# Batch 1's score stacks built by selection products, batch 0's maxima subtracted by a product, and a new order of steps

## The chip, the cores and the metric

The kernel runs on one core of a Trainium2 chip. The metric is the device time of one execution in microseconds (us); lower is better. The engines are TensorE (PE, with its weight loads as PEld), VectorE (DVE), ScalarE (ACT), GpSimd (POOL) and SyncE (SP, which issues all transfers; its queue is SPq).

## The reference

16 batches of 256 tokens x 128 channels pass through one attention layer and one mixture-of-experts layer, each between layer norms and with a residual:

```python
qkv = einsum('bnc,ce->bne', layernorm(x), w_qkv)         # 16 heads of 8 channels
attn = softmax(einsum('bhnd,bhmd->bhnm', q, k) / sqrt(128))
x = x + layernorm(einsum('bhnm,bhmd->bhnd', attn, v) @ w_out)
xf = layernorm(x)
rw = weights of the 2 best of 8 experts of xf @ Wr + bias # softmax over the two
ffn = sum_e rw[e] * (silu(xf @ Wg[e]) * (xf @ Wu[e])) @ Wd[e] + silu(xf @ Sg) * (xf @ Su) @ Sd
x = x + layernorm(ffn)
```

## The kernel before

One batch is one unit of work, cut into about 100 named steps. The table `TIMES` gives each step of each batch a tick; every engine runs its own steps in the order of the ticks and waits on semaphores for what they need. So the table is the whole order: a step's place on its engine is its tick, and steps of three or four batches are mixed. A step's name with a batch in brackets, `s1_3(1)`, is what the text below uses.

Attention works with heads in pairs (`s` = 0 to 7, two heads of rows 0 to 47 and 64 to 111). q and k are split in three bf16 parts (`part1`, `part2`, `part3`, on ScalarE, ScalarE and GpSimd, with `rest1` on VectorE), and six products of parts stand as six groups of 8 rows in the stacks `qs` and `ks`: 48 rows per head. Scores are made twice: `s1` (L630) has queries on the output partitions and feeds `max` (L1011), which finds each query's maximum; `s2` (L646) has keys there and feeds `exp` (L860). In `s2` the maxima are subtracted by three more rows of the stacks: `ks` holds -1 there (`load_minus`), `qs` the maxima, split in three by `msplit` (GpSimd), transposed by `maxT` (L684), copied by `max_copy` (L867) and brought in by the transfers of `max_stack` (L558). `pv` (L662) multiplies with v. The score banks `sc` are two; `s1` and `s2` steps take them in turn, so each waits for the `max` or `exp` of the step before the last.

The stacks of a batch are made by transfers: `spill` writes `parts` to DRAM in 6 transfers (L541, L544), `stack` reads it back in 4 (L551, L553). Batch 0's stacks are made without them, since nothing is there to hide the way: `sel1`, `sel2`, `sel3`, `selq` (L739 to L752) multiply `parts[0]` with selection matrices `lay`, and `kl_copy`, `ql_copy`, `kh_copy`, `qh_copy` bring the results to `ks` and `qs`. `lay` lies in the memory of `hidden` and is made by `lay0a`, `lay0b`, `lay1`, `lay2`.

`FILL`, `FILL_SCORES` and `FILL_LAST` put filler products of the identity (L669, L611, L673) ahead of named steps; one filler is two instructions of the trace. One f32 product is two instructions of the trace, a bf16 product one.

## Time and profile before

| | us |
|---|---|
| median of 3 runs | 373.94 |
| lowest and highest | 372.68, 377.52 |
| the profiled execution | 373.3 |
| its span in the trace | 371.5 |
| TensorE busy | 347.3 (93%) |
| VectorE busy | 312.9 (84%) |
| ScalarE busy | 267.4 (72%) |
| GpSimd busy | 200.5 (54%) |
| granted TensorE clock, mean | 0.988 |

The span is the time from the first to the last instruction in the trace; 1.8 us of the execution's time lie around it. Busy shares are means over stages with different limits: the start has attention alone, the middle attention and experts of different batches, the end experts alone.

### The profile page before, as it was taken

The numbers are of one execution on the slowest core, as the hardware profiler recorded it, in microseconds if no ns is written. First come the engines' busy times: TensorE is split into PE (matmuls) and PEld (weight loads), VectorE is DVE, ScalarE is ACT, GpSimd is POOL, SyncE is SP. The second block draws the span as 40 slices with busy tenths as digits, with TensorE's granted clock in tenths as the row PEclk, the third lists the DMA queues.
The fourth block names the chain that finished last, engine by engine and source line by source line (L and its number), as shares of the span: only waits on it lengthen the run. The fifth ranks groups of instructions, "written<-read, shape, count | busy, mean of one in ns | idle before, by whom it ended". The sixth has DMA issues, their size and how long they took to land.

```text
span 371.5 us, 9933 instructions
## 1 busy us (share of the span) xinstructions
PE 347.3 (93%) x3244; PEld 222.8 (60%) x3244; DVE 312.9 (84%) x788; ACT 267.4 (72%) x511; POOL 200.5 (54%) x518
## 2 busy tenths in 40 slices
PE   8987888999999999999998999999999999998892
PEld 7855444454475657575756565665765566677772
DVE  8696588989989999999888999999998987667661
ACT  4752578689779778969885896788778968864522
POOL 7333051424566454776656365754773576767654
PEclk9998799999999999999999999999999999999998
DMA  2256858663377456355566565386364240422210
GB/s 84 66 136 149 209 119 188 146 145 113 108 183 159 142 127 164 79 144 161 131 170 140 145 125 158 103 199 149 86 185 103 66 129 27 123 62 72 58 31 29
DMA packets 59921, 45.64 MB, mean 123 GB/s; under 512 B 8966, under 2 KB 56966, under 8 KB 59870
## 3 DMA queue, kind: packets, MB, share of 16 engines
q1 hardware_dynamic: 59870, 45.00, 48.3%
q8 instruction: 26, 0.43, 0.5%
q14 instruction: 25, 0.20, 0.2%
HBM read 26.69 MB, written 17.81 MB: 120 GB/s over the span
## 4 chain that ended last, share of the span: by engine, by line
PE 59%; issue 10%; DVE 10%; POOL 7%; ACT 5%; DMA 5%; SPq 3%; POOLq 0%; DVEq 0%; ACTq 0%
PE pvp L662 10%; PE bank_d L832 8%; PE bank_d L816 8%; PE sc L646 7%; DVE mx L1011 6%; PE bank_d L817 6%; PE sc L630 5%; PE bank_a L715 3%; PE bank_d L669 2%; PE bank_d L789 2%; POOL hidden L1220 2%; ACT pr L860 2%; PE sc L611 2%; DMA ks<-qk_dram 2%; POOL rstd L1153 1%
## 5 line engine op out<-in xcount | busy, mean ns | idle before, releaser
L1011 DVE TENSOR_REDUCE mx<-sc 128x4 f32<-128x1024 f32 x128 | 154.3, 1217 | 18.7 <-PE sc L630 17.7
L860 ACT ACTIVATE pr<-sc 128x1024 f32<-128x1024 f32 x128 | 130.8, 1024 | 27.4 <-PE sc L646 26.6
L662 PE MATMUL pvp<-pr,va 128*32 128x256 f32 x1024 | 68.5, 385 | 0.0
L816 PE MATMUL bank_d<-x3T,wg_sb 128*128 128x256 f32 x160 | 54.2, 420 | 2.8 <-DVE hidden L1109 1.9
L630 PE MATMUL sc<-ks,qs 48*128 48x256 bf16 x512 | 50.0, 274 | 3.4 <-DVE mx L1011 1.9
L646 PE MATMUL sc<-qs,ks 51*128 51x256 bf16 x512 | 50.1, 276 | 1.8 <-DMA qs<-mT 1.3
L1220 POOL TENSOR_TENSOR hidden<-hidden,rwb 128x256 f32<-128x256 f32 x60 | 42.2, 729 | 11.0 <-DMA rwb<-rw_dram 10.2
L817 PE MATMUL bank_d<-x3T,wu_sb 128*128 128x256 f32 x160 | 47.6, 379 | 0.0
L1153 POOL TENSOR_TENSOR rstd<-vareps,mhalf 128x2 f32<-128x2 f32 x64 | 44.5, 696 | 0.0
L662 PEld LDWEIGHTS pvp<-pr,va 128*32 128x32 f32 x1024 | 26.7, 109 | 25.1 <-issue 12.4
L943 ACT ACTIVATE th<-bank_d 128x256 f32<-128x256 f32 x80 | 30.5, 382 | 14.8 <-PE bank_d L817 12.8
L832 PE MATMUL bank_d<-wd_sb,hidden 128*128 128x128 f32 x320 | 39.2, 278 | 0.4 <-POOL hidden L1220 0.2
L1103 DVE SCALAR_TENSOR_TENSOR ha<-th,bank_d 128x256 f32<-128x256 f32 x80 | 32.3, 406 | 8.6 <-ACT th L943 8.1
L832 PEld LDWEIGHTS bank_d<-wd_sb,hidden 128*128 128x128 f32 x320 | 37.1, 192 | 3.2 <-issue 2.5
L1148 POOL TENSOR_TENSOR vareps<-mv,eps 128x2 f32<-128x2 f32 x64 | 12.5, 195 | 45.3 <-DVE mv L994 42.8
L646 PEld LDWEIGHTS sc<-qs,ks 51*128 51x128 bf16 x512 | 16.1, 95 | 32.7 <-issue 14.5
L816 PEld LDWEIGHTS bank_d<-x3T,wg_sb 128*128 128x128 f32 x160 | 24.1, 188 | 18.9 <-issue 18.3
L1109 DVE SCALAR_TENSOR_TENSOR hidden<-ha,bank_d 128x256 f32<-128x256 f32 x80 | 32.8, 412 | 1.6 <-PE bank_d L832 0.6
L817 PEld LDWEIGHTS bank_d<-x3T,wu_sb 128*128 128x128 f32 x160 | 30.4, 190 | 4.1
L1164 POOL TENSOR_TENSOR parts<-rest,parts 128x512 bf16<-128x512 f32 x16 | 18.5, 1157 | 26.7 <-ACT parts L888 26.7
L630 PEld LDWEIGHTS sc<-ks,qs 48*128 48x128 bf16 x512 | 18.7, 95 | 23.0 <-DVE mx L1011 7.2
L1043 DVE RECIPROCAL rden<-den 128x256 f32<-128x256 f32 x14 | 24.4, 1745 | 2.4 <-DMA den<-pv_dram 2.4
(115 smaller groups left out, 495.7 us busy)
## 6 DMA issues: line engine op xcount, KB each, us to landing
rwb<-rw_dram SPq DMA_DIRECT2D x30, 256.0 KB, 4.3
qk_dram<-parts SPq DMA_DIRECT2D x30, 192.0 KB, 2.7
qs<-qk_dram SPq DMA_DIRECT2D x30, 192.0 KB, 4.1
ks<-qk_dram SPq DMA_DIRECT2D x30, 192.0 KB, 4.6
qk_dram<-parts SPq DMA_DIRECT2D x30, 128.0 KB, 2.5
pv_dram<-pv_sb SPq DMA_DIRECT2D x14, 256.0 KB, 2.4
x_sb<-in_L_attn_x_dram SPq DMA_DIRECT2D x16, 128.0 KB, 2.7
out_dram<-x SPq DMA_DIRECT2D x16, 128.0 KB, 1.8
```

What stands on the lines that cost most here:

```text
L630: mm = pe.matmul(sc[pair][:, u, c, :], q[rows, s, c * P:(c + 1) * P], k[rows, s, :], start=True, stop=True)
L646: mm = pe.matmul(sc[pair][:, u, c, :], k[rows, s, c * P:(c + 1) * P], q[rows, s, :], start=True, stop=True)
L662: mm = pe.matmul(pvp[32 * j:32 * j + 32, g, :], values[:, X * c + 4 * g + j, 32 * tt:32 * tt + 32], pr[:, k, c * N:(c + 1) * N], start=(tt ...
L816: pe.matmul(bank_d[bank][:, 0:N], wg_sb[:, ORDER[n], :], x3T[b % 2][:], start=True, stop=True)
L817: pe.matmul(bank_d[bank][:, N:2 * N], wu_sb[:, ORDER[n], :], x3T[b % 2][:], start=True, stop=True).then_inc(gu_done, 1)
L832: mm = pe.matmul(bank_d[0][:, c * P:(c + 1) * P], src, wd_sb[:, n, :], start=(n == 4), stop=(n == 3))
L860: nc.scalar.activation(pr[:, 2 * s:2 * s + 2, :].rearrange("p k n -> p (k n)"), sc[PAIR["s2", b, s]][:].rearrange("p u c n -> p (u c n)"), ...
L1011: nc.vector.tensor_reduce(mx[b % 2][:, :, :, s].rearrange("p c u -> p u c"), sc[PAIR["s1", b, s]][:], AX.X, ALU.max).then_inc(max_done, 1)
L1103: nc.vector.scalar_tensor_tensor(out=ha[n][:], in0=th[n][:], scalar=1.0, in1=bank_d[BANK[n]][:, 0:N], op0=ALU.add, op1=ALU.mult).then_inc( ...
L1109: nc.vector.scalar_tensor_tensor(out=hb[b % 2][:, ORDER[n], :], in0=ha[n][:], scalar=0.5, in1=bank_d[BANK[n]][:, N:2 * N], op0=ALU.mult, o ...
L1153: nc.gpsimd.tensor_tensor(rstd[L][p][:], vareps[L][p][:], mhalf[:], ALU.pow).then_inc(rstd_done[L], 1)
L1220: nc.gpsimd.tensor_tensor(hw[b % 2][:, n, :].rearrange("p (t g r) -> p t g r", t=TT, g=4), hb[b % 2][:, n, :].rearrange("p (t g r) -> p t ...
```

## The change

- Batch 1 has no `spill` and no `stack`. Eight steps `u0` to `u7` on TensorE make its stacks: each multiplies `parts[1]` with `lay` for two head pairs, the even ones for `ks` into bank `bank_d[0]`, the odd ones for `qs` into `pvp`. Eight copies `uc0` to `uc7` on ScalarE bring them over. `u_j` waits for `uc_(j-2)`; `s1_s(1)` with even `s` waits for `s + 2` copies.
- Batch 0 has no `max_stack`. `maxT(0)` puts the two halves of the maxima at rows 0 and 64, `max_copy(0)` is two copies, and each `s2` step of batch 0 has four products of 48 rows and four more of 24 rows that add `msel` (-1 in the rows of the step's head) times `mT[0]` to the same bank. `msel` is a new table, made by GpSimd.
- `load_minus` waits for all copies of batch 1, and batch 1's `s2` waits for it.
- Every tick of the table is new; fillers are fewer.

The core of the diff:

```diff
-    "maxT": {0: 7},
+    "maxT": {0: 1},
     "qk": {0: 1},
     "sel1": {0: 2},
-    "xT": {0: 17, 3: 4},
+    "xT": {0: 17},
 }
 FILL_SCORES = {
-    ("s1", 0, 2): 1,
-    ("s1", 0, 3): 1,
-    ("s1", 1, 3): 1,
-    ("s1", 1, 4): 2,
-    ("s1", 2, 7): 1,
-    ("s1", 3, 6): 1,
+    ("s1", 2, 1): 2,
+    ("s1", 3, 7): 1,
     ("s2", 0, 0): 2,
-    ("s2", 0, 4): 2,
-    ("s2", 0, 5): 1,
-    ("s2", 1, 3): 2,
+    ("s2", 1, 1): 1,
 }
...
                 sp.wait_ge(kh_copied, 2)
+                sp.wait_ge(unit_copied, 8)
...
-                if (b := due(tick, "spill")) is not None and b:
+                if (b := due(tick, "spill")) is not None and b >= 2:
...
-                if (b := due(tick, "stack")) is not None and b:
+                if (b := due(tick, "stack")) is not None and b >= 2:
...
-                if (b := due(tick, "max_stack")) is not None:
-                    sp.wait_ge(max_copied, b + 1)
+                if (b := due(tick, "max_stack")) is not None and b:
+                    sp.wait_ge(max_copied, b + 2)
...
+                if b == 1 and s % 2 == 0:
+                    pe.wait_ge(unit_copied, s + 2)
...
                 if s == 0:
-                    pe.wait_ge(max_stacked[b % 2], landed(2, b))
                     if b == 0:
+                        pe.wait_ge(max_copied, 2)
+                        pe.wait_ge(msel_done, 6)
+                    else:
+                        pe.wait_ge(max_stacked[b % 2], landed1(2, b))
+                    if b == 1:
                         pe.wait_ge(minus_load, DMA * 2)
...
-                        rows = slice(64 * u, 64 * u + ROWS_MAX)
-                        mm = pe.matmul(sc[pair][:, u, c, :], k[rows, s, c * P:(c + 1) * P], q[rows, s, :], start=True, stop=True)
+                        rows = slice(64 * u, 64 * u + (ROWS_MAX if b else ROWS))
+                        mm = pe.matmul(sc[pair][:, u, c, :], k[rows, s, c * P:(c + 1) * P], q[rows, s, :], start=True, stop=b > 0)
+                    if b == 0:
+                        for u in range(2):
+                            rows = slice(64 * u, 64 * u + 3 * X)
+                            mm = pe.matmul(sc[pair][:, u, c, :], msel[rows, s:s + 1].broadcast_to([3 * X, P]), mT[0][rows], start=False, stop=True)
...
+                for j in range(8):
+                    if due(tick, f"u{j}") is not None:
+
+                        pe.wait_ge(part3_done, 2)
+                        if j < 2:
+                            pe.wait_ge(qh_copied, 2)
+                        else:
+                            pe.wait_ge(unit_copied, j - 1)
+                        bank = bank_d[0][0:WIDTH].rearrange("p (x n) -> p x n", x=2) if j % 2 == 0 else pvp[0:WIDTH]
+                        q = 1 - j % 2
+                        for x in range(2):
+                            for n in range(3):
+                                mm = pe.matmul(bank[:, x, :], lay[:, n, q, 2 * (j // 2) + x, :], parts[1][:, q, n, :], start=(n == 0), stop=(n == 2))
+                        mm.then_inc(unit_done, 1)
+                        if j == 6:
+                            d_empty[0] = (unit_copied, 7)
...
+                for j in range(8):
+                    if due(tick, f"uc{j}") is not None:
+                        act.wait_ge(unit_done, j + 1)
+                        bank = bank_d[0][0:WIDTH].rearrange("p (x n) -> p x n", x=2) if j % 2 == 0 else pvp[0:WIDTH]
+                        dst = qs[1][0:WIDTH] if j % 2 else ks[0:WIDTH, 1]
+                        nc.scalar.copy(dst[:, 2 * (j // 2):2 * (j // 2) + 2, :], bank).then_inc(unit_copied, 1)
```

The new order of the steps at the start, on the engines that the prediction speaks of:

- TensorE: xT(0) qk(0) sel1 v(0) sel2 xT(1) sel3 qk(1) selq xT(2) s1_0(0) s1_1(0) v(1) u0 s1_2(0) u1 s1_3(0) qk(2) u2 s1_4(0) s1_5(0) u3 v(2) u4 s1_6(0) u5 s1_7(0) xT(3) u6 s1_0(1) u7 s1_1(1) qk(3) s1_2(1) s1_3(1) maxT(0) s2_0(0) xT(4) s1_4(1) s2_1(0) v(3) s2_2(0) s1_5(1) qk(4) s2_3(0) s1_6(1) pv_0(0) s2_4(0) s2_5(0) pv_1(0) s2_6(0) s1_7(1) pv_2(0) s2_7(0) s1_0(2) s1_1(2) maxT(1)
- Before: ... s1_3(0) qk(2) s1_4(0) xT(3) s1_5(0) v(2) s1_6(0) s1_7(0) qk(3) maxT(0) s1_0(1) s1_1(1) v(3) s1_2(1) xT(4) s1_3(1) s2_0(0) s1_4(1) s2_1(0) qk(4) s2_2(0) s1_5(1) pv_0(0) s2_3(0) s1_6(1) s2_4(0) s1_7(1) s2_5(0) pv_1(0) s1_0(2) s2_6(0) pv_2(0) maxT(1) s2_7(0) s1_1(2)
- SP after the change: load_x(0) load_x(1) load_x(2) load_wd load_wgu load_x(3) load_wout load_x(4) load_x(5) load_x(6) spill(2) stack(2) spill(3) load_minus load_x(7) max_stack(1) stack(3)

## Rows read from the trace of the kernel before

**Rows 1.** View by stretches; the second number is the stretch's length, x counts instructions.

```profile
core 0: us, PE busy (x) PEld busy (x) DVE busy (x) ACT busy (x) POOL busy (x), PEclk, DMA share, GB/s
...
18.00:30.00 12.00, 10.94 (x82) 7.18 (x80) 10.77 (x15) 6.76 (x16) 4.18 (x12) 1.00 0.59 133
30.00:42.00 12.00, 9.57 (x56) 5.87 (x58) 6.33 (x7) 3.49 (x6) 2.46 (x3) 0.72 0.65 148
42.00:60.00 18.00, 14.41 (x164) 6.64 (x159) 14.98 (x22) 13.36 (x21) 5.63 (x17) 1.00 0.79 186
...
50.00:60.00 10.00, 8.03 (x84) 3.65 (x76) 9.39 (x16) 8.07 (x16) 4.72 (x13) 1.00 0.67 158
...
60.00:340.00 280.00, 274.36 (x2686) 169.44 (x2686) 250.65 (x630) 222.41 (x417) 161.36 (x418) 1.00 0.52 130
340.00:371.50 31.50, 22.51 (x162) 18.98 (x162) 16.28 (x69) 10.84 (x30) 17.11 (x44) 0.96 0.12 35
```

**Rows 2.** Chain of waits, 14 to 60 us: start, us, what.

```profile
22.96 1.64 DMA qk_dram<-parts
...
25.92 5.81 DMA ks<-qk_dram
...
31.87 0.41 PE sc L630 x4
...
37.74 1.15 PE sc L611 x4
```

**Rows 3.** List of waits, 18 to 62 us: us in total, times, longest.

```profile
PE sc L630 <- DMA ks<-qk_dram: 1.2, 1, 1.2
```

**Rows 4.** The page's transfers: count, size, median us to landing.

```profile
ks<-qk_dram SPq DMA_DIRECT2D x30, 192.0 KB, 4.6
```

**Rows 5.** Timeline, 16 to 31 us: start, us, engine, line; idle before.

```profile
16.91 0.86 PE L752 MATMUL pvp<-parts,hidden 128*112 128x256 bf16 x6 [0.29 <-ACT ks L895]
17.23 1.04 ACT L891 CAST ks<-sc 112x1024 bf16<-112x1024 f32 x1
17.61 0.82 PE L752 MATMUL bank_d<-parts,hidden 128*112 128x256 bf16 x6
...
18.86 1.15 POOL L1164 TENSOR_TENSOR parts<-rest,parts 128x512 bf16<-128x512 f32 x1 [5.41 <-ACT parts L888]
...
21.57 0.59 ACT L898 CAST qs<-pvp 112x512 bf16<-112x512 f32 x1
...
27.87 1.22 DVE L1011 TENSOR_REDUCE mx<-sc 128x4 f32<-128x1024 f32 x1
...
28.17 1.72 PE L669 MATMUL bank_d<-ident 128*128 128x128 f32 x14
...
30.04 0.24 POOL L1185 TENSOR_TENSOR mp<-mrest,mp 128x32 bf16<-128x32 f32 x1
```

**Rows 6.** Timeline, 37 to 58 us.

```profile
37.13 0.61 PE L646 MATMUL sc<-qs,ks 51*128 51x256 bf16 x4
...
39.79 1.95 PE L715 MATMUL bank_a<-xT,wqk_sb 128*128 128x256 f32 x4
...
41.67 0.39 PE L646 MATMUL sc<-qs,ks 51*128 51x256 bf16 x4
...
41.90 0.38 PE L630 MATMUL sc<-ks,qs 48*128 48x256 bf16 x4
...
42.22 1.07 PE L662 MATMUL pvp<-pr,va 128*32 128x256 f32 x16
...
50.83 1.02 ACT L860 ACTIVATE pr<-sc 128x1024 f32<-128x1024 f32 x1
...
57.47 1.13 PE L715 MATMUL bank_a<-xT,wqk_sb 128*128 128x256 f32 x4
```

**Rows 7.** Timeline at 14.8 us: statistics of batches 3 and 4.

```profile
14.76 0.81 DVE L987 BATCH_NORM_STATS2 st<-x_sb 128x6 f32<-128x128 f32 x4
```

**Rows 8.** List of waits, whole span.

```profile
PE sc L646 <- DMA qs<-mT: 1.3, 1, 1.3
```

More of the change, by code:

```diff
@@ L55 @@
[L55 to L64 removed]
+    "load_x": [0, 12, 17, 40, 62, 65, 67, 181, 290, 312, 373, 441, 489, 514, 656, 904],
@@ L65 @@
+    "load_wout": [43],
[5 rows of a table added]
+    "v_copy": [50, 84, 102, 152, 201, 274, 363, 517, 607, 692, 840, 944, 1066, 1206, 1324, 1441],
+    "pickm": [51],
+    "sel3": [53],
+    "minusm": [55],
     "ql_copy": [59],
     "kh_copy": [60],
-    "selq": [62],
-    "kl_copy": [63],
[4 rows of a table removed]
-    "spill": [None, 74, 123, 143, 193, 253, 341, 455, 576, 680, 830, 947, 1018, 1165, 1258, 1403],
-    "s1_2": [75, 122, 179, 247, 319, 418, 536, 630, 734, 862, 973, 1102, 1209, 1318, 1437, 1549],
-    "qh_copy": [80],
[5 rows of a table removed]
-    "stack": [None, 92, 137, 186, 221, 295, 420, 483, 633, 785, 887, 991, 1084, 1244, 1320, 1448],
[3 rows of a table removed]
@@ new lines @@
+    "uc0": [81],
+    "u1": [82],
+    "max_2": [85, 133, 195, 257, 335, 434, 535, 644, 751, 857, 988, 1112, 1228, 1325, 1439, 1567],
+    "s1_3": [86, 130, 196, 263, 340, 430, 538, 647, 758, 867, 992, 1118, 1232, 1336, 1445, 1569],
+    "uc1": [87],
+    "max_3": [89, 137, 200, 265, 345, 442, 543, 652, 768, 872, 996, 1123, 1236, 1342, 1448, 1578],
+    "u2": [90],
+    "s1_4": [92, 141, 202, 268, 347, 446, 546, 658, 774, 884, 1006, 1145, 1237, 1346, 1462, 1591],
+    "uc2": [94],
+    "s1_5": [95, 154, 209, 273, 356, 457, 565, 662, 787, 897, 1031, 1160, 1251, 1356, 1475, 1597],
@@ L297, in sandwich @@
         mrest = ring(2, "mrest", [P, TT, 2, X])
-        mT = ring(2, "mT", [3 * H, N], BF16)
+        mT = ring(2, "mT", [64 + 3 * X, N], BF16)
+        msel = sb("msel", [64 + 3 * X, X], BF16)
         pr = sb("pr", [P, H, TT * N])
```

207 lines of the change are left out of this document (126 added, 81 removed), and 142 rows, old and new, of the table TIMES.

## The prediction

> **What bounds the kernel now.** I read the view by stretches first, because TensorE is the fullest engine of the page and a share over the whole span hides where it is not full. From 60 to 340 us it works 274.36 of 280 us [rows 1]: 98%, 5.6 us idle. That stage can't get much shorter without less work on TensorE. From 340 us on it is idle for 9.0 us, in the chain of the last batch, which the change doesn't touch. What is left is the start: from 18 to 60 us TensorE is idle for 1.06 + 2.43 + 3.59 = 7.1 us, and in 30 to 42 us the granted clock is 0.72, so part of the work runs at 1.2 GHz in place of 2.4. So the account is: span = TensorE work at full clock + what the half clock adds + idle time. Everything that starts TensorE's full stage earlier shortens the span by that much, as long as no work is added.
>
> The chain of waits says what holds the start [rows 2]: the end of the six spill transfers of batch 1 (landed at 24.6), then the stack load, 5.81 us on its last piece, then `s1_0(1)` at 31.87. The wait list agrees and gives the size: TensorE's own wait for that load is 1.2 us, once [rows 3]. Behind it the filler products (L611) stand in the chain, at half clock. A batch's transfers normally take less: 4.6 us to landing for `ks<-qk_dram` [rows 4].
>
> The timeline shows the two things that have to be compared. Before the load lands the maxima of batch 0 run on VectorE, back to back to 29.09, then the split on GpSimd (done 30.28), `maxT`, `max_copy` and the `qs<-mT` transfer [rows 5]. `s2_0(0)` starts at 37.13 and `exp_7(0)` at 50.83 [rows 6]. It starts behind `s1_3(1)` in TensorE's order, and the wait that ended last there was not the transfer's.
>
> **The change, part by part.** *Transfers out.* Batch 1 loses 6 spills and 4 stack loads, and batch 0 its two `max_stack` rows: 12 issues less on SP's queue, each just under 0.5 us. Only the 1.2 us wait is on the path. `stack(2)` and `spill(3)` move up behind them; in the new order `s1_0(2)` has 8.5 us of TensorE work between it and `stack(2)`, where batch 1 had 3.2. I cost this part at nothing beyond the 1.2 us, and it can only help.
>
> *Selection products in.* Eight steps `u0` to `u7` of 6 products each. The same products of batch 0 (`selq`) are the L752 row: 6 in 0.86 us, the next 6 start 0.70 later [rows 5]. So 8 x 0.70 to 8 x 0.86 = 5.6 to 6.9 us of TensorE (6.1 in the sum), and eight copies of 0.59 us (L898) = 4.7 us on ScalarE. ScalarE is busy 6.76 of 12 us from 18 to 30 [rows 1], so its copies fit. TensorE is the engine that doesn't hide them. I walk through the new order with the durations of before: `u0` needs `part3(1)` (20.02) and `qh_copy` (behind `kl_copy`), so it starts at 20.3. From there to the end of `s1_3(1)` TensorE has eight units 6.9, ten `s1` steps at 0.39 = 3.9, `qk(2)` and `qk(3)` 2.2, `v(2)` 0.7, `xT(3)` 0.4: 14.1 us, which ends at about 34.3. Batch 0's maxima, which in before set the pace, now wait for TensorE: `s1_4`, `s1_6` and `s1_7` stand behind units, and `max_7(0)` ends at about 30.7, 1.6 later than the 29.09 of before. `s1_0(1)` needs only `uc1` and a free bank and starts at about 30.8, 1.1 earlier. The fourth maximum of batch 1, `max_3(1)`, ends at about 37.2; in before it ends at 37.32. So the gain of the missing transfer is eaten up to here by the units.
>
> *Batch 0's maxima by a small product.* The split ends at 31.9, but `maxT(0)` now stands behind `s1_3(1)` and needs the bank that `rest1(3)` frees (about 34.8), and the copy in two halves is 0.7: `max_copied` 36.0. `s2_0(0)` also needs `max_2(1)` to free its bank (36.0) and has 2 fillers: it starts at 36.6, 0.5 before the 37.13. Each of the eight `s2` steps doubles from 4 products to 8. The trace has no 24-row product. Nearest rows: 4 more of the same kind are 0.22 us when they run in pairs (41.67 to 41.90 in [rows 6]) and at most the whole step again, 0.39. So +1.8 to +3.1 us on TensorE; I take 0.33 a step, 2.6, because the pairs have to follow each other into the same bank. A bound below nothing has no mechanism: products are only added.
>
> *Fillers out.* `xT(3)` loses 4 and `maxT(0)` 6 (20 instructions at 0.11 at full clock, from 14 in 1.72 [rows 5]: 2.2 us), the score steps fall from 14 to 6. The 14 took 7.1 us over their rows of the timeline, some at half clock as the 1.15 at 37.74 [rows 2]; 6 at full clock are about 1.5. So 5.6 less. It is a gain only where real work takes their place, which is why the idle time is counted beside it.
>
> *Half clock.* In 30 to 42 us `qk(4)` took 1.95 us against the 1.13 of `qk(5)` at full clock, and six score steps 0.61, as the one at 37.13, against 0.39 [rows 6]: 0.8 + 1.3 = 2.1 us. What came before the fall was TensorE waiting for the stack load. By my walk TensorE has no such gap between 20 and 34 us, so I count the 2.1 as gained. If the clock falls all the same in 35 to 45 us, where there are gaps of 0.7 and 0.8 us and fewer fillers, it stays.
>
> *Sum of work.* -2.2 - 5.6 - 2.1 + 6.1 + 2.6 = -1.2 us of TensorE. Idle time from 18 to 60 us goes from 7.1 to about 6: 0.3 until 34, 2.0 from 34 to 38, under 1 until 50, then 3 as before, because from 50 to 60 VectorE is busy 9.39 of 10 us with the maxima of batch 2 [rows 1], and that stays. By this count the span falls by 2.3 us.
>
> *Cross-check by the chain.* From `s2_0(0)` to `exp_7(0)` TensorE has 8 x 0.72 = 5.8, four `s1` 1.6, `xT(4)`, `v(3)`, `qk(4)` 2.2, three `pv` of 1.07 = 3.2: 12.8 us, of which some 0.3 overlaps, against 13.7 in before. `exp_7(0)` starts at about 49.1, 1.7 us earlier. The maxima of batch 2, though, start with `s1_0(2)` at about 49.2, no earlier than the 48.6 of before, since the new order puts it behind `s2_7(0)`. ScalarE and TensorE gain 1.7, VectorE nothing; from 60 to 340 us VectorE is at 90% and TensorE at 98% [rows 1], so TensorE's gain is the one that counts. I take 1.7 us, between the chain's 1 to 2 and the account's 2.3.
>
> *The rest moved.* Ten weight loads go ahead of `load_x(3)` on SP's queue, under 5 us; `x(3)` then lands near 11, and its statistics were at 14.76 [rows 7]. `lay1` behind the first `xT_copy` puts `part1(0)` some 0.15 later, and `msel` (a fill and six small selects) takes GpSimd's place of `pickm` and `minusm`, which go behind `part3(0)`. Until `sel2` nobody waits for any of it, so nothing; if that cover is thin, it costs the 0.15. The steps after 60 us are in a new order with the same work. Its limits are the 5.6 us of idle there: all of it gone is -5.6, as much again is +5.6. With 98% of TensorE full and the same work, I take 0. I looked for close pairs: the smallest distance from `stack` to `s1_0` is now 7.9 us of TensorE work (3.2 before), from `max_copy` to `s2_0` 3.6 from batch 1 on, from `max_7(1)` to `maxT(1)` 1.2 (the split takes 1.15). Nothing is clearly late.
>
> *Changes of shape.* In [rows 6] a score step followed by another starts it 0.23 us later (41.67, 41.90), followed by `pv`, whose products have another shape, 0.32 later (41.90, 42.22): 0.1 more per change. The Trainium skill, TensorEngine Tiling (Array Packing), section Key Properties, says that a change of tiling mode drains TensorE. By that rule the pairs of 48 and 24 rows in `s2` would each pay it; the row agrees with a small price.
>
> **The rivals.** (1) *The units take the place of the transfer, and the clock falls later* (slower side). VectorE is what lags: `max_7(0)` is 1.6 us later, and if units take the 0.86 plus a change of shape on both sides (0.2 x 8), 3.2 later. With gaps of 0.7 us around 35 and no fillers, the clock falls for 36 to 48 us: some 9 us of work there at half speed adds up to 4. It decides when the granted clock stays under 1 for more than the 8 us it does now. Price +1.6 + 1.6 + 2 to 4 over no gain: 378 to 381, at the most 382. For: the clock fell in before on a gap of about 1.2 us. Against: TensorE's 14.1 us of unbroken work just before. (2) *The new order after 60 us decides*, for the better: 3 to 5.6 us of its idle go, with my 1.7: 366.6 to 369. For: `s2` waiting 1.3 us on `qs<-mT` once [rows 8] is an order fault that a new order can mend. Against: it can make others. (3) *Changes of shape*: each `s2` step of batch 0 goes 48, 24, 48, 24 rows, three changes more than before: 24 x 0.1 = 2.4 us in a stretch where TensorE has under 1 us free: the 1.7 turns to +0.7, 374.6. (4) *It moves nothing*: the transfer was hidden but for 1.2 us and the units cost that; VectorE's maxima, no earlier for batch 2, stay the bound: 373.5 to 374.5.
>
> **How the numbers follow.** The profiled execution took 373.3 us for a span of 371.5; the median of the three is 373.94, 0.6 above it. 371.5 - 1.7 = 369.8 of span, 371.6 for that execution, and 373.9 - 1.7 = 372.2 as a median. Chances: forecast (371 to 373.4) 0.36, rival 1 0.15, rival 2 0.20, rival 3 0.13, rival 4 0.16. Over 2% is 7.5 us, about what a measurement of this kernel can tell from no change: under 366.5 or over 381.4. Rival 2 reaches the first with a third of its chance, and rival 1 the second with a third of its own. Range 367 to 379: it leaves out rival 2's best and rival 1's worst. Faster 0.08, same 0.87, slower 0.05.
>
> **What would show it.** Right: no `ks<-qk_dram` in the chain before 45 us; `u0` at 20.3 and `max_7(0)` ending near 30.7; granted clock above 0.9 in 30 to 42 us; `s2_0(0)` at 36 to 37 and `exp_7(0)` near 49; TensorE still 98% from 60 to 340 us; TensorE's total busy time within 2 us of 347. Wrong: a long step of 8 products in `s2` (over 0.9 us), a clock under 0.8 after 35 us, VectorE waiting on `s1` for more than 1 us at a time between 20 and 30 us, or idle time after 60 us other than 4 to 8 us.

## The result, and the profile of the changed kernel

The changed kernel takes 389.65 us (median of 4 runs, 389.42 to 391.16), the kernel before 374.8 us in the same comparison (median of 4). The ratio is 1.040, with an interval of 1.032 to 1.048: 4% slower. The forecast was 372.2, its range 367 to 379. The profiled execution has a span of 388.0 us against 371.5, 16.5 us longer, and this is the difference that has to be found. (Executions over 1.5% longer than the fastest of the same kernel are left out of the ratios, for e17_rows48_old752 five of twelve, so a ratio can differ a little from the quotient of two medians.)

The view by stretches of the changed kernel, to be read against [rows 1]:

```profile
core 0: us, PE busy (x) PEld busy (x) DVE busy (x) ACT busy (x) POOL busy (x), PEclk, DMA share, GB/s
18.00:30.00 12.00, 11.70 (x102) 8.35 (x99) 11.66 (x15) 7.82 (x17) 3.52 (x10) 1.00 0.01 2
30.00:42.00 12.00, 10.55 (x64) 5.21 (x62) 7.16 (x12) 6.91 (x12) 4.35 (x10) 0.72 0.67 155
42.00:60.00 18.00, 17.42 (x123) 6.00 (x126) 6.22 (x8) 7.34 (x10) 2.07 (x5) 0.50 0.16 42
60.00:220.00 160.00, 154.81 (x1562) 91.46 (x1556) 148.38 (x337) 127.79 (x233) 83.79 (x223) 0.99 0.58 146
220.00:300.00 80.00, 74.09 (x697) 48.14 (x694) 69.04 (x171) 59.95 (x115) 44.72 (x113) 0.98 0.52 130
300.00:340.00 40.00, 39.09 (x375) 23.94 (x374) 32.37 (x97) 30.88 (x59) 24.66 (x65) 1.00 0.28 76
340.00:388.00 48.00, 36.46 (x273) 28.81 (x272) 25.65 (x106) 20.58 (x52) 28.11 (x70) 0.95 0.19 52
```

And the granted clock of the page, 40 slices of 9.7 us:

```profile
PEclk9998557999999999999999999999999999999997
```

The row to stop at is 42 to 60 us. TensorE counts as busy for 17.42 of 18 us, fuller than before (14.41), and its clock is 0.50 for the whole stretch: 1.2 GHz. VectorE works 6.22 us of the 18. The busy share alone would be read as good news. By stretches of 3 us the clock is 1.00 until 35, 0.55 in 35 to 38, 0.50 until 62 and 0.90 in the next one: 27 us at half clock, where the kernel before had some 7.

The account of the 16.5 us: the page's total of TensorE's busy time is 359.4 us against 347.3, so 12.1 more. Its idle time from 18 to 60 us fell from 7.1 to 0.30 + 1.45 + 0.58 = 2.3, so 4.8 less. From 60 to 340 us it is 5.19 + 5.91 + 0.91 = 12.0 against 5.6, so 6.4 more, nearly all of it in 220 to 300 us (there it was 0.65). Behind 340 us it is 11.5 against 9.0, 2.5 more; ahead of 18 us 0.2 more. 12.1 - 4.8 + 6.4 + 2.5 + 0.2 = 16.4.

The same by the progress of the batches. In each kernel `exp_7(b)`, ScalarE's last exponential of batch b, starts at (us):

| batch | 0 | 1 | 10 | 12 | 15 | end |
|---|---|---|---|---|---|---|
| before | 50.8 | 67.8 | 234.6 | 274.5 | 329.9 | 371.5 |
| changed | 55.6 | 75.3 | 241.5 | 289.2 | 343.4 | 388.0 |
| later by | 4.8 | 7.5 | 6.9 | 14.7 | 13.5 | 16.5 |

So there are two losses, with 160 us of even running between them: 7.5 us in the first 75, and 7.8 us between batches 10 and 12 (39.9 us before, 47.7 now), with 3 more behind `exp_7(15)` (41.6 us before, 44.6 now). One cause doesn't do for both.

The start of the first loss, in the timeline of the changed kernel (start, duration, engine and line, operation, shape):

```profile
19.30 0.83 PE L804 MATMUL bank_d<-parts,hidden 128*112 128x256 bf16 x6 [0.29 <-ACT qs L970]
20.07 0.39 PE L653 MATMUL sc<-ks,qs 48*128 48x256 bf16 x4
20.39 0.86 PE L804 MATMUL pvp<-parts,hidden 128*112 128x256 bf16 x6
...
33.88 0.28 PE L673 MATMUL sc<-qs,ks 48*128 48x256 bf16 x2
34.09 0.28 PE L677 MATMUL sc<-mT,msel 24*128 24x256 bf16 x2
34.30 0.28 PE L673 MATMUL sc<-qs,ks 48*128 48x256 bf16 x2
34.52 0.28 PE L677 MATMUL sc<-mT,msel 24*128 24x256 bf16 x2
34.73 0.44 PE L743 MATMUL bank_a<-ident,xn 128*128 128x128 f32 x2
...
42.23 0.40 PE L673 MATMUL sc<-qs,ks 48*128 48x256 bf16 x2
42.56 0.39 PE L677 MATMUL sc<-mT,msel 24*128 24x256 bf16 x2
42.89 0.40 PE L673 MATMUL sc<-qs,ks 48*128 48x256 bf16 x2
43.22 0.39 PE L677 MATMUL sc<-mT,msel 24*128 24x256 bf16 x2
43.54 0.61 PE L653 MATMUL sc<-ks,qs 48*128 48x256 bf16 x4
44.08 1.93 PE L695 MATMUL pvp<-pr,va 128*32 128x256 f32 x16
...
55.56 1.02 ACT L916 ACTIVATE pr<-sc 128x1024 f32<-128x1024 f32 x1 [2.69 <-PE sc L677]
```

Up to `s2_0(0)` all is as early as forecast or earlier: `u0` at 19.30, `s2_0(0)` at 33.88 (37.13 before, [rows 6]). The first step of eight products takes 33.88 to 34.73, 0.85 us, at full clock; at half clock, as at 42.23, 1.31. The starts of its pairs (x2 in the rows) are 0.21 us apart at full clock and 0.33 at half. In the kernel before, one whole step of four products followed another by 0.23 us [rows 6], so a pair took about 0.11.

The second loss, in the timeline of SP, GpSimd, VectorE and TensorE:

```profile
214.14 0.54 SPq L603 DMA_DIRECT2D rw_dram<-rwT  x1
...
217.35 0.44 SPq L565 DMA_DIRECT2D qk_dram<-parts  x1
217.89 1.26 SPq L610 DMA_DIRECT2D rwb<-rw_dram  x2
...
224.15 2.10 POOL L1300 TENSOR_TENSOR hidden<-hidden,rwb 128x256 f32<-128x256 f32 x3 [5.19 <-DMA rwb<-rw_dram]
...
249.87 0.17 DVE L1168 RECIPROCAL gp<-g 128x2 f32<-128x2 f32 x1 [2.34 <-POOL g L1281]
250.49 0.66 PE L853 MATMUL bank_d<-ident,x 128*128 128x128 f32 x2 [2.23 <-DVE hidden L1180]
```

The weights of the experts go out to memory (`rw_dram`) and come back (`rwb`), and six spill transfers of a later batch stand between the two in SP's queue (in the kernel before that is so for one of the three batches in this stretch, here for both); GpSimd waits 5.19 us for `rwb`, later VectorE for GpSimd and TensorE for VectorE. The list of waits between 205 and 262 us has GpSimd waiting for `rwb` 8.6 us in all, against 2.5 in the same stretch of before. That is one candidate.

### The profile page after: what moved, and what is told of

Read it like the earlier page. It is cut to its first block, busy times and chain, and to the rows that moved or that the text cites. A ratio compares the mean times of both kernels' runs of the same rounds, so it can differ in the third digit from the quotient of the medians.

```text
span 388.0 us, 10047 instructions
## 1 busy us (share of the span) xinstructions
PE 359.4 (93%) x3290; PEld 225.9 (58%) x3290; DVE 312.5 (81%) x788; ACT 272.8 (70%) x520; POOL 202.3 (52%) x525
## 4 chain that ended last, share of the span: by engine, by line
PE 39%; POOL 22%; issue 20%; DVE 9%; ACT 5%; SPq 2%; DMA 2%; POOLq 1%; DVEq 0%; ACTq 0%
PE pvp L695 7%; POOL hidden L1300 5%; POOL rstd L1224 5%; PE sc L673 5%; PE sc L653 4%; PE bank_d L872 4%; DVE mx L1082 4%; PE bank_d L888 4%; PE bank_d L873 3%; PE bank_a L753 2%; ACT pr L916 2%; POOL x L1276 2%; PE bank_a L763 1%; POOL x L1307 1%; POOL vareps L1219 1%
## 5 line engine op out<-in xcount | busy, mean ns | idle before, releaser
L916 ACT ACTIVATE pr<-sc 128x1024 f32<-128x1024 f32 x128 | 130.8, 1025 | 34.2 <-PE sc L673 23.6
L695 PE MATMUL pvp<-pr,va 128*32 128x256 f32 x1024 | 72.0, 401 | 0.0
L872 PE MATMUL bank_d<-x3T,wg_sb 128*128 128x256 f32 x160 | 54.2, 420 | 2.0 <-DVE hidden L1180 1.6
L673 PE MATMUL sc<-qs,ks 51*128 51x256 bf16 (+1 forms) x512 | 52.6, 280 | 3.6 <-DMA qs<-mT 1.8
L653 PE MATMUL sc<-ks,qs 48*128 48x256 bf16 x512 | 50.8, 280 | 0.7 <-DVE mx L1082 0.3
L888 PE MATMUL bank_d<-wd_sb,hidden 128*128 128x128 f32 x320 | 40.5, 283 | 4.9 <-POOL hidden L1300 4.9
L1224 POOL TENSOR_TENSOR rstd<-vareps,mhalf 128x2 f32<-128x2 f32 x64 | 44.6, 697 | 0.0
L888 PEld LDWEIGHTS bank_d<-wd_sb,hidden 128*128 128x128 f32 x320 | 38.6, 198 | 8.0 <-issue 4.5
L673 PEld LDWEIGHTS sc<-qs,ks 51*128 51x128 bf16 (+1 forms) x512 | 16.9, 94 | 38.1 <-issue 20.2
```

What stands on the lines that cost most here:

```text
L653: mm = pe.matmul(sc[pair][:, u, c, :], q[rows, s, c * P:(c + 1) * P], k[rows, s, :], start=True, stop=True)
L673: mm = pe.matmul(sc[pair][:, u, c, :], k[rows, s, c * P:(c + 1) * P], q[rows, s, :], start=True, stop=b > 0)
L695: mm = pe.matmul(pvp[32 * j:32 * j + 32, g, :], values[:, X * c + 4 * g + j, 32 * tt:32 * tt + 32], pr[:, k, c * N:(c + 1) * N], start=(tt ...
L872: pe.matmul(bank_d[bank][:, 0:N], wg_sb[:, ORDER[n], :], x3T[b % 2][:], start=True, stop=True)
L888: mm = pe.matmul(bank_d[0][:, c * P:(c + 1) * P], src, wd_sb[:, n, :], start=(n == 4), stop=(n == 3))
L916: nc.scalar.activation(pr[:, 2 * s:2 * s + 2, :].rearrange("p k n -> p (k n)"), sc[PAIR["s2", b, s]][:].rearrange("p u c n -> p (u c n)"), ...
```

## The experiments

Theories at the start. A: the 24-row products between 48-row ones are dear, by the change of shape, by the half clock, or both (a product's shape is here the number of rows of the array that it uses). B: the fillers that were taken out held the clock. C: the new order of the late steps makes the second loss. "Old order behind tick N" means: the new table up to tick N, then the remaining steps in the sequence of the kernel before. Where the base is the kernel before, the part is put into it alone.

All runs, in groups; `exp_7(0)` is the start of that step and 10 to 12 the time between `exp_7(10)` and `exp_7(12)`, both read in the one profiled execution, whose own time stands beside the median:

| run | base and edit | median us | profiled us | ratio to before, interval | exp_7(0) | 10 to 12 |
|---|---|---|---|---|---|---|
| changed | | 389.65 | 389.81 | 1.040 [1.032, 1.048] | 55.6 | 47.7 |
| e2_without_msel | changed, no subtraction | 380.17 | 384.13 | 1.012 [1.003, 1.020] | 47.2 | 47.9 |
| e1_fill_old | changed, all old fillers | 383.01 | 382.20 | 1.020 [1.010, 1.030] | 50.9 | 44.6 |
| e6_front_fill | changed, 10 old fillers | 387.01 | 387.37 | 1.027 [1.016, 1.038] | 55.4 | 44.3 |
| e8_dense_msel | changed, 128 rows | 383.15 | 380.46 | 1.027 [1.019, 1.035] | 50.9 | 44.8 |
| e13_rows48 | changed, 48 rows | 378.25 | 381.19 | 1.010 [1.002, 1.019] | 48.4 | 45.0 |
| e3_before_few_fill | before, new fillers | 376.09 | 376.04 | 1.007 [1.004, 1.011] | 52.1 | 39.9 |
| e5_msel_alone | before + 24 rows | 387.59 | 388.13 | 1.038 [1.030, 1.046] | 62.8 | 40.0 |
| e9_before_dense | before + 128 rows | 384.09 | 381.25 | 1.032 [1.025, 1.040] | 58.0 | 40.3 |
| e18_before_rows48 | before + 48 rows | 378.16 | 378.01 | 1.011 [1.006, 1.016] | 54.2 | 40.1 |
| e12_units_alone | before + units | 383.68 | 383.81 | 1.026 [1.019, 1.032] | 62.3 | 39.9 |
| e4_tail_old | changed, old order behind 200 | 387.04 | 387.33 | 1.031 [1.024, 1.038] | 55.5 | 40.0 |
| e7_w_load | changed, two loads moved | 391.16 | 391.45 | 1.045 [1.037, 1.053] | 57.0 | 45.6 |
| e10_dense_old200 | e8, old order behind 200 | 377.74 | 376.94 | 1.016 [1.009, 1.023] | 49.3 | 40.2 |
| e15_dense_old752 | e8, old order behind 752 | 377.66 | 377.58 | 1.009 [1.005, 1.014] | 52.3 | 40.1 |
| e11_dense_old1000 | e8, old order behind 1000 | 377.61 | 381.33 | 1.011 [1.005, 1.017] | 52.2 | 40.2 |
| e14_dense_old200_fill | e10 + nine fillers | 384.72 | 385.20 | 1.027 [1.019, 1.036] | 51.2 | 40.5 |
| e16_sparse_old200_fill | e4 + all old fillers | 381.46 | 383.47 | 1.020 [1.011, 1.028] | 51.3 | 40.0 |
| e17_rows48_old752 | e13, old order behind 752 | 376.38 | 379.23 | 1.000 [0.995, 1.004] | 49.8 | 40.1 |

### The first loss: fillers, or the product?

**e1_fill_old** puts the fillers of before back into the changed kernel, **e6_front_fill** only those of `maxT(0)` and `xT(3)`, **e3_before_few_fill** takes them out of the kernel before.

```
-    "maxT": {0: 1},          -    "xT": {0: 17},
+    "maxT": {0: 7},          +    "xT": {0: 17, 3: 4},     (e6: these alone)
+FILL_SCORES = {('s1', 0, 2): 1, ..., ('s2', 0, 4): 2, ... ('s2', 1, 3): 2}   (e1: the ten entries of before as well)
```

> The changed kernel in its new order, with the fillers of the kernel before. Three theories for the granted clock of 0.5 from 35 to 62 us (it was 0.5 from 35 to 41 before). Fillers: it is their loss that keeps the clock down; then it is back at 1.0 by about 45 us as before, exp_7(0) starts near 49 to 51 (55.6 changed), and the time falls by 6 to 8 us, to 381 to 384; the rest above the kernel before is the stall at 220 to 262 us. Products: the sparse 24-row products keep it down whatever fills the gaps; then the clock stays at 0.5 to 60 and the fillers only add work: 390 to 393. Order: the place of the steps does it; 389 to 392.

> The changed kernel with only the fillers ahead of maxT(0) (7 for 1) and xT(3) (4 for none) put back, none of the eight in the score steps. If it is enough that the clock doesn't fall at 35 us, it stays at 1.0 to 60 us and exp_7(0) starts near 50: 381 to 384, as with all fillers. If the fillers between the score steps are what keeps or restores it, it is at 0.5 from 35 or 40 us to 60: 388 to 391.

> The kernel before, with the fillers of the changed one (maxT(0) 1 for 7, xT(3) none, six for 14 in the score steps). Fillers theory: the clock falls at about 33 us and stays at 0.5 well past 41 us, to 55 or later: 379 to 384. Products theory and order theory: it comes back near 41 us as before: 372 to 375.

e1 regains 2% of the 4. Its clock is 1.00 until 59 us:

```profile
30.00:42.00 12.00, 11.80 (x94) 7.37 (x92) 8.44 (x15) 7.06 (x14) 4.16 (x11) 1.00 0.56 134
42.00:60.00 18.00, 16.04 (x173) 7.62 (x172) 11.93 (x15) 11.31 (x16) 3.88 (x10) 0.99 0.45 105
```

The fall at 35 us is absent. The fillers close the gaps of TensorE ahead of it. 30 to 35 us, the changed kernel first, e1 second, and third e10_dense_old200, a run from further below without these fillers:

```profile
30.00:35.00 5.00, 3.88 (x32) 2.03 (x30) 4.07 (x6) 2.83 (x7) 2.04 (x5) 1.00 0.57 161
```

```profile
30.00:35.00 5.00, 5.00 (x42) 3.49 (x40) 4.76 (x9) 1.26 (x3) 2.45 (x6) 1.00 0.55 158
```

```profile
30.00:35.00 5.00, 3.88 (x32) 2.12 (x30) 4.07 (x6) 2.68 (x6) 2.08 (x5) 1.00 0.56 160
```

With 1.12 us of idle time there the clock falls in the changed kernel, with none it doesn't in e1. But e10 has the same 1.12 us, and its clock stays at 1.00 until 62 us. e8, e10, e11 and e15 (all below) have the same instructions on TensorE in the same order up to 48 us, and the clock falls at 33.9 us for 3.4 us, not at all, and at 34.3 us for 6.8 us in the last two. So the gaps come before the fall where it comes, but they don't settle whether it comes, and one profiled execution is thin evidence for it. In 42 to 60 us TensorE completes 173 instructions in 16.04 busy us, where the changed kernel completed 123 in 17.42. But B is not the cause by itself: the kernel before without these fillers (e3) loses 0.7%, though its clock is 0.50 from 24 to 44 us; and e6, with ten of them ahead of the first s2 step, has its clock at 1.00 until 40 us only, at 0.50 for 20 us behind that, and is still 2.7% slower than before. So the fillers cover something that the kernel before doesn't have.

**e2_without_msel** leaves out the subtraction of batch 0's maxima (the four 24-row products of each s2 step); its output lacks that part.

```
-                    if b == 0:
-                        for u in range(2):
-                            rows = slice(64 * u, 64 * u + 3 * X)
-                            mm = pe.matmul(sc[pair][:, u, c, :], msel[rows, s:s + 1].broadcast_to([3 * X, P]), mT[0][rows], start=False, stop=True)
```

> The changed kernel without the 32 products that subtract the maxima of batch 0: that subtraction is left out. It takes 1.3 us per score step at half clock, 10.5 us in all, off TensorE. Products theory: the clock comes back by 45 us and the time falls by over 10 us, to 376 to 380. Fillers theory: the clock stays down as long as the score steps of batch 0 last, but there is less work in it, so the stretch ends earlier: 382 to 385, with 0.5 to about 54 us.

380.17 us, 9.5 less by medians, and `exp_7(0)` at 47.2, 8.4 us earlier. The clock falls here too, at 34.2 us, but is back at 41 us. A step with the 24-row products takes 0.85 us at full clock and 1.31 at half; the four products alone take 0.39 and 0.61 [rows 6]. That is at most 0.7 us in each of eight steps, 5.6 us in all; the rest of the 8.4 goes with the other work, which runs at half clock until 62 us in the changed kernel. Which part of the 9.5 us of the total comes from where isn't separated. **e5_msel_alone** asks the reverse: the 24-row product in the kernel before, with its order, its stack of batch 1 and its fillers.

> The kernel before, its order and its fillers, with one part of the change: the maxima of batch 0 by the product of 24 rows, no max_stack(0). Theory A (the sparse products by themselves keep the clock down once it has fallen at 33 us): 0.5 to 55 us or later, 381 or more. Theory B (they only add work, and the fillers bring the clock back): the clock is back by 46 us, exp_7(0) 1 to 3 us later than 50.8, 375 to 377.

387.59 us: this part alone, in the old order and with the old fillers, costs nearly all that the whole change costs. Its rows show the same picture, clock 0.50 (from 33 to 67 us by the trace's record of the clock) under a TensorE that is busy 16.84 of 18 us:

```profile
30.00:42.00 12.00, 10.06 (x57) 5.61 (x58) 6.33 (x7) 3.06 (x7) 2.46 (x3) 0.62 0.63 153
42.00:60.00 18.00, 16.84 (x110) 6.48 (x113) 6.52 (x11) 6.09 (x7) 1.41 (x7) 0.50 0.39 97
```

So the product is the place of the first loss. What in it is dear?

### Small product, or change of shape?

**e8_dense_msel** and **e9_before_dense** run the product over all 128 rows (zeros in the rows that don't count); the result is the same sum. If smallness lost the clock, this keeps it; the shape still changes.

```
-        mT = ring(2, "mT", [64 + 3 * X, N], BF16)
-        msel = sb("msel", [64 + 3 * X, X], BF16)
+        mT = ring(2, "mT", [P, N], BF16)
+        msel = sb("msel", [P, 2, X], BF16)
...
-                            mm = pe.matmul(..., msel[rows, s:s + 1].broadcast_to([3 * X, P]), mT[0][rows], ...)
+                            mm = pe.matmul(..., msel[:, u, s:s + 1].broadcast_to([P, P]), mT[0][:], ...)
```

> The changed kernel with the subtraction of batch 0's maxima as products over all 128 rows (the rows that don't count are zero), four a score step as before but not in pairs, so some 0.2 us more each step at full clock. If it is the few rows in use that keep the clock at 0.5 from 35 to 62 us, it comes back by 48 us and the time is 380 to 386. If rows don't matter and only fillers or the work between them do, it stays at 0.5 and the added work costs 2 to 3 us: 391 to 394.

> The kernel before, its order and fillers, with batch 0's maxima subtracted by a product over all 128 rows (the others zero) where the run with 24 rows gave 387.6. Rows theory: the clock comes back by 46 us and the products cost only their own time, 8 x 0.65 us with part of it free: 375 to 378. If the extra products of any shape hold the clock down in this order: 386 to 392.

The clock comes back: it is 1.00 from 37 us in e8, and in e9 0.91 on average from 42 to 60 us. Yet e9 is still 3.2% slower than before. Its timeline shows a part of the reason:

```profile
42.80 0.28 PE L654 MATMUL sc<-qs,ks 48*128 48x256 bf16 x2
43.02 0.39 PE L657 MATMUL sc<-mT,msel 128*128 128x256 bf16 x2
43.34 0.28 PE L654 MATMUL sc<-qs,ks 48*128 48x256 bf16 x2
43.56 0.39 PE L657 MATMUL sc<-mT,msel 128*128 128x256 bf16 x2
43.88 0.39 PE L634 MATMUL sc<-ks,qs 48*128 48x256 bf16 x4
```

The 48-row pair takes 0.22 us to the next start, as in the changed kernel, and the 128-row products 0.32: two in a row at 0.11 each, and 0.1 more. A step is 1.08 us, at full clock. So the half clock is one part of the loss, and the longer step, with its changes of shape, another.

**e13_rows48** and **e18_before_rows48** make the product 48 rows high, in the same two row halves as the scores: no change of shape, the same number of products as with 24 rows.

```
-        mT = ring(2, "mT", [64 + 3 * X, N], BF16)
+        mT = ring(2, "mT", [WIDTH, N], BF16)
...
-                            rows = slice(64 * u, 64 * u + 3 * X)
-                            mm = pe.matmul(..., msel[rows, s:s + 1].broadcast_to([3 * X, P]), mT[0][rows], ...)
+                            rows = slice(64 * u, 64 * u + ROWS)
+                            mm = pe.matmul(..., msel[rows, s:s + 1].broadcast_to([ROWS, P]), mT[0][rows], ...)
...
+                    nc.gpsimd.memset(mT[0][:], 0.0).then_inc(msel_zeroed, 1)
```

> The changed kernel with the subtraction as products of 48 rows in pairs, as the score products beside them: 24 rows that count and 24 of zeros. It costs no more time than 24 rows do. Shape theory (what holds the clock down is the change between two shapes, or the drain at it): without the change the clock comes back by 48 us and the time is 380 to 384. Rows theory (few rows in use, over the stretch): 48 rows are still under half of the array, so it stays at 0.5 past 55 us, 386 to 391.

> The kernel before with the subtraction part alone, as pairs of 48 rows (24 rows gave 387.6, 128 rows 384.1 in this order). If the change of shape was the whole price of that part: eight steps cost 0.22 us more each, the clock is back by 44 us as in the kernel before, exp_7(0) at 51 to 53 and the time 374 to 377. If this order can't take any product more: over 380.

e13 takes 378.25 us: 11.4 less than the changed kernel, and the largest step of the study. e18 takes 378.16, 9.4 less than the same with 24 rows (e5). A whole step of e13 at full clock, and its stretches:

```profile
42.04 0.28 PE L673 MATMUL sc<-qs,ks 48*128 48x256 bf16 x2
42.16 0.27 PE L677 MATMUL sc<-mT,msel 48*128 48x256 bf16 x2
42.27 0.27 PE L673 MATMUL sc<-qs,ks 48*128 48x256 bf16 x2
42.38 0.27 PE L677 MATMUL sc<-mT,msel 48*128 48x256 bf16 x2
42.49 0.38 PE L653 MATMUL sc<-ks,qs 48*128 48x256 bf16 x4
...
30.00:42.00 12.00, 10.88 (x71) 6.02 (x68) 8.07 (x15) 6.90 (x12) 5.16 (x13) 0.72 0.55 134
42.00:60.00 18.00, 15.96 (x187) 8.21 (x186) 13.64 (x16) 12.81 (x18) 3.28 (x9) 1.00 0.57 141
```

The same eight products take 0.45 us in place of 0.85. Twice the rows, half the time: the 0.10 us that each pair has on top of 0.11 is the price of the change, not of the product. At half clock the pairs of e13 are 0.21 apart (its starts at 37.13, 37.34 and 37.56) against 0.33 with 24 rows: 0.12. In 42 to 60 us 187 instructions complete. The clock falls in both kernels at 35 us (e13 has the same 3.88 us of work in 30 to 35 as the changed kernel), but here it is back at 41.5 us and not at 62.6.

What keeps the clock down in the changed kernel is not the change of shape alone, though e13 by itself reads so. e11 and e15 have as many changes with 128 rows, their clock falls at 34.3 us as well, and it is back at 41.1, in the middle of such a step (e11):

```profile
40.62 0.61 PE L676 MATMUL sc<-mT,msel 128*128 128x256 bf16 x2
41.16 0.28 PE L673 MATMUL sc<-qs,ks 48*128 48x256 bf16 x2
41.38 0.39 PE L676 MATMUL sc<-mT,msel 128*128 128x256 bf16 x2
```

The half clock lasted 20 to 34 us in the five kernels where it fell near the steps with 24-row products (changed, e4, e5, e6, e7), 3 to 7 us with 128-row products and as many changes (e8, e9, e11, e15), and 7 to 10 us with 48 rows and no change (e13, e17, e18). Few rows together with changes is what the long stretches have in common. A run with few rows and no change would separate the two, and there is none. With all the old fillers and 24 rows (e1, e16) the clock didn't fall there at all. With the old order of the kernel before, the ratios have the same order: 24 rows 1.038, 128 rows 1.032, 48 rows 1.011. Both e9 and e18 are slower than was expected for the theory that they bear out (384.09, not 375 to 378; 378.16, not 374 to 377), so in this order the added products cost some 4 us even with 48 rows, and no run says how.

**e12_units_alone** puts the selection products of batch 1 into the kernel before and keeps the stack rows of the maxima.

```
+    "u0": [81.2],      "uc0": [81.3], ...   (between the steps of batch 0's maxima)
-    "load_minus": [101],
+    "load_minus": [104.5],
...
+                sp.wait_ge(unit_copied, 8)      (ahead of load_minus)
```

> The kernel before, its order and fillers, with the other part of the change alone: batch 1's stacks by eight steps of selection products, maxima of batch 0 still as stack rows (so load_minus and max_stack(0) come behind the last copy, at about 33 us). Dense products of 128 rows: the clock should stay at 1.0 until the units end. Against the transfer they cost 5.6 to 6.9 us of TensorE and free a wait of 1.2 us: exp_7(0) between 50 and 54 us, 373 to 378. If units hold the maxima back more than I worked out, above 379.

2.6% slower, `exp_7(0)` at 62.3. This can't be read as the price of the units: `load_minus`, which writes rows of the same `ks`, has to wait for the last of them (40.3 us) and `max_stack(0)` is issued behind it at 43.1, so the maxima of batch 0 come through the queue late. The clock also falls twice, at 31 and at 55 us, for 7 us each. The run shows only that the units and the stack rows of batch 0 don't go together in this order. What the units cost with the other parts in place is not separated.

### The second loss: the order of the late steps

**e4_tail_old**: the changed kernel with the old order behind tick 200.

```
-    "w_load": [413, 593, 743, 839, 943, 1078, 1186, 1322, 1393, ...],
-    "spill": [None, None, 128, 165, 206, 275, 400, 468, 600, ...],
+    "w_load": [405, 614, 727, 826, 936, 1065, 1183, 1302, 1398, ...],
+    "spill": [None, None, 116, 153, 196, 256, 343, 457, 578, ...],
...     (all steps)
```

> The changed kernel in its new order up to exp_7(0) and the first score steps of batch 2 (the first 200 ticks), all later steps in the order of the kernel before. If the stall at 220 to 262 us (7 to 8 us between exp_7(10) and exp_7(12)) and the 2 us at the end are the new order's own, they go: 379 to 382, with exp_7(0) still at 55.6 and a loss of 7 to 8 us that is there by batch 1. If the late stall is a late effect of the slow start, it stays: 388 to 390.

From 10 to 12 it takes 40.0 us, as before: the second loss is gone, so C holds. The same column of the table says it for all runs: 39.9 to 40.5 us in the thirteen kernels with the old order there, 44.3 to 47.9 in the seven with the new one. The highest of these, 47.7 and 47.9 (changed and e2), are the two whose clock also fell for 3.4 us in that stretch, at 250 and at 242 us; without such a fall it is 44.3 to 45.6. So of the changed kernel's 7.8 us some 4 to 6 are the order's, and the rest comes with that fall. Behind `exp_7(15)` the new order also takes longer, 44.6 to 47.1 us, against 41.6 to 42.9 with the old one. The total gains only 2.6 us, because some 4 us are lost where the two orders join (`exp_7(1)` at 79.4 against 75.3). **e7_w_load** moves only what the timeline had pointed at, `w_load` ahead of the spills:

```
-    "w_load": [..., 1078, 1186, ...],
+    "w_load": [..., 1055.5, 1163.5, ...],
```

> The changed kernel with two steps moved on SyncE's queue: w_load(5) and w_load(6) ahead of the six transfers of spill(12) and spill(13) that stood between w_spill and w_load. If GpSimd's waits for rwb (5.2 and 3.4 us at 219 and 241 us) make the late stall, exp_7(10) to exp_7(12) takes 41 to 44 us in place of 47.7 and the time is 383 to 386, with the start as slow as it was. If they hide behind other waits: 389 to 391.

GpSimd's waits for `rwb` between 205 and 262 us fall from 8.6 to 4.5 us, and the time doesn't: 391.16, with 12.5 us idle behind 340. The 45.6 us from 10 to 12 are 2.1 less than in the changed kernel, but no less than in the other new-order runs without the fall of the clock there. So no gain by the moved loads is shown.

**e10_dense_old200**, **e15_dense_old752** and **e11_dense_old1000** are e8 with the joint at three places.

> The changed kernel with the products over all 128 rows, in the new order for its first 200 ticks and in the old one behind. The old order took 39.9 us from exp_7(10) to exp_7(12), the new one 44.9 with these products. If the late loss is the order's: 40 us there again and, with 3 to 4 us lost where the orders meet, 378 to 382; if it is something else of the changed kernel, 383 as with the new order.

> Products over 128 rows, the new order up to tick 752 (the attention of batch 6) and the old one behind: asks where in the new order the late loss is made. exp_7(10) to exp_7(12) at 40 us as in both earlier mixes (200 and 1000), idle time of TensorE from 80 us on at 5 to 7 us as in the kernel before: 376 to 379. If the new order is also worse from 60 to 180 us, this is 2 us above the mix at 200.

> The same with the new order up to tick 1000 (through most of batch 8's attention) and the old one behind. If the loss of the middle comes from the order between 220 and 300 us alone, exp_7(10) to exp_7(12) takes 40 to 41 us and the time is 376 to 380. If it is built up earlier (steps that are already late at tick 1000), it stays above 43 us there and at 381 to 384 in all.

All three have 40.1 to 40.2 us from 10 to 12 and come to 377.6 or 377.7, 5.5 us less than e8 by medians (by the ratios 1.1 to 1.8%, 4 to 7 us). The row of e15 for 220 to 300 us against that of the changed kernel, above, shows the place: 0.91 us idle, not 5.91.

```profile
60.00:220.00 160.00, 152.62 (x1540) 90.83 (x1542) 148.13 (x342) 128.46 (x237) 84.58 (x226) 1.00 0.56 145
220.00:300.00 80.00, 79.09 (x783) 49.27 (x775) 75.59 (x186) 64.73 (x123) 47.57 (x119) 1.00 0.52 131
300.00:340.00 40.00, 39.99 (x354) 26.19 (x354) 29.15 (x106) 30.28 (x61) 27.24 (x72) 1.00 0.29 79
```

As a joint at tick 1000 does as well as one at 200, the fault lies behind tick 1000, roughly the attention from batch 9 on and the experts from batch 6 on. The joint itself has a price that moves with it: 60 to 220 us has 7.4 us idle in e15 and 8.6 in e11, 5.2 in the changed kernel.

**e14_dense_old200_fill** adds nine fillers to e10, eight of them of the kernel before and four of these already at 28 us (`xT(3)`), to lift the dip of the clock at its joint (0.50 from 62.9 us for 6.8 us), **e16_sparse_old200_fill** all of them to e4:

```
+    'xT': {..., 3: 4};  FILL_SCORES: ('s1', 2, 7): 1, ('s1', 3, 6): 1, ('s2', 1, 3): 2, ('s2', 1, 5): 1 added     (e14)
+    the FILL and FILL_SCORES tables of before     (e16)
```

> The run with products over 128 rows and the old order behind tick 200 (377.7), with the fillers of the kernel before back in xT(3) and in the score steps of batches 1 to 3. That run had its clock at 0.5 to 0.7 from 62 to 71 us, behind a gap at 56 to 62. If that fall is the fillers' loss, it goes and the time is 374 to 376; if not, 377 to 379.

> The changed kernel's own products of 24 rows, all fillers of the kernel before, and the old order behind tick 200: both causes mended without touching the products. The fillers kept the clock at 1.0 from 30 to 59 us in the new order. 376 to 379; over 382 would mean that one of the causes is wrong.

e14 is a miss: 384.72, 7 us more, with the clock at 0.50 from 62 to 76 us, and `exp_7(1)` at 77.0 against 71.8. More fillers didn't hold the clock, and why it fell there isn't explained. e16 misses its range too (381.46, not 376 to 379): it gains 5.6 us on e4, its clock is 1.00 until 64 us, and it is still 2% slower than before.

**e17_rows48_old752** takes both repairs: 48 rows, and the old order behind tick 752.

> Both causes mended: the changed kernel with the subtraction as pairs of 48 rows (378.3 in the new order) and the old order behind tick 752. The old order behind took 5.5 us off the version with 128 rows (383.15 to 377.7), and 48 rows take 3.8 us less than 128 at exp_7(0). If both add up: 372 to 375, at the kernel before or just under it. If the start's gain doesn't last: 376 to 378.

Ratio 1.000, interval 0.995 to 1.004. Its twelve executions lie between 371.0 and 379.5 us with a median of 376.38, those of the kernel before in the same comparison between 371.7 and 378.1 with a median of 373.41. So most of the 15 us are gone and nothing is won: the median misses the 372 to 375 that was expected, and lies in the range given for a gain that doesn't last. That is the best version of the change, and it is not shown to beat the kernel before.

## Why the prediction was wrong

Three steps of the prediction failed, and each had a rival or a bound that was given too little.

**The half clock was counted as gained** ("By my walk TensorE has no such gap between 20 and 34 us, so I count the 2.1 as gained"). The walk was right up to 30 us (TensorE idle 0.30 us from 18 to 30); then the gaps that I had put at 34 to 38 us came at 30 to 35, 1.12 us of them, and the clock fell at 35 us, as my own proviso said, and stayed down for 27 us. TensorE's total busy time came to 359.4 us, 12.1 more than before, where the sum had 1.2 less. Rival 1 had the fall and its reason, gaps and missing fillers; it put 9 us of work and at most 4 us on it. (Its terms add up to 379.1 to 381.1 us, not 378 to 381.) What it missed is how long the clock stays down: with the same gaps and fillers, e13 is back at full clock at 41.5 us and e11 at 41.1. What they lack is the 24-row products with a change of shape on either side; which of the two properties does it is open. And it isn't seen as idle time, since the busy share counts these steps as work.

**The s2 step was sized too small.** I took 0.72 us a step, 0.33 of it for the four added products, by the old rows. It measured 0.85 at full clock and 1.31 at half, where seven of the eight steps ran: 1.0 us more than forecast for eight steps at full clock, 4.3 more as they ran. The nearest row for such products was right: with 48 rows the step takes 0.45 (e13). Wrong was to leave the change of shape outside that term. Rival 3 priced it at 0.1 us each, and the trace agrees: 0.10. It counted three changes a step, 24 in all; a step goes into 24 rows and out of them twice, up to 32 in all, 3.2 us. Alone the 1.0 us would leave the forecast inside its range; together with the clock the 24 rows put `exp_7(0)` 7.2 us later than in e13 (55.6, 48.4). The Trainium skill, TensorEngine Tiling (Array Packing), section Key Properties, says that a change of tiling mode drains TensorE; the trace agrees, 0.10 us a change at full clock and 0.12 at half.

**"The steps after 60 us are in a new order with the same work ... I take 0"** failed too. Its upper bound was 5.6 us, "as much again"; TensorE was idle 6.4 us more between 60 and 340 us and 2.5 more behind that; by medians the new late order costs 5.5 us (e8 against e10). The pairs of steps that I checked for distance were right (`stack` to `s1_0`, `max_copy` to `s2_0`), but `w_load` to the step that reads it was not among them, though e7 doesn't show that moving it gains anything. A sum of work can't price an order, and rival 2 priced the better side alone, though it says that a new order can make faults.

What held: no `ks<-qk_dram` in the chain before 45 us, and an early start: `u0` was forecast at 20.3 and came at 19.30; the end of `max_7(0)` was forecast at 30.7 and came by 28.6, when the split behind it starts; `s2_0(0)` was forecast at 36.6 and came at 33.88. What didn't: the clock in 30 to 42 us was 0.72, not above 0.9; `exp_7(0)` came at 55.56, not 49.1; and the end of the last batch, "which the change doesn't touch", took 3 us longer. With 48 rows `exp_7(0)` is at 48.4, near the forecast, but partly by luck: the clock fell there too, for 6.8 us, and the shorter step and the early start made up for it. Idle time from 18 to 60 us went to 2.3, not 6, and bought nothing. The sign that I had named for the wrong case, a step of eight over 0.9 us and a clock under 0.8 after 35 us, is what came.

Why e17 gains nothing, though `exp_7(0)` is 1.0 us earlier than in before, isn't shown by a run of its own. In its profiled execution (span 376.2 us) TensorE is busy 350.0 us against 347.3, since units and added products are its work where the kernel before left it to the DMA queues, and 10 us at half clock go into the same number. It is idle 3.2 us from 18 to 60 us against 7.1, but 9.4 from 60 to 220 us against 4.6, and this stretch holds the joint.

**Open.** Why the clock falls at 34 to 36 us in some executions and not in others with the same instructions; whether few rows or changes of shape make it stay down; which of the late steps behind tick 1000 costs the 5.5 us; why the joint of e14 was worse with more fillers; what the units cost with the rest in place; and, of the 11.4 us between 24 and 48 rows, how much the changes cost by themselves and how much through the clock. With 128 rows in the old order the loss is 12 us (e9) against 4 with 48 rows (e18), although the clock was down for 10 us in both. 8 steps at 1.08 in place of 0.45 are 5.0 us of the 8 between them: an estimate that leaves most of that gap to the longer step.
